# Summing attention weights over edges: VectorE adds half of every group's slots before TensorE's identity matmuls

## What is computed

```python
w_m = (efeat @ W_msg + b_msg).reshape(E, in_f, -1)     # [E, 16, 16]
w_a = (efeat @ W_attn + b_attn).reshape(E, in_f, -1)
h_src = feat[src][:, :, None]
e1, e2 = w_m * h_src, w_a * h_src
ex = jnp.exp(e2 - seg_max[dst])
denom = segment_sum(ex, dst)
ft = segment_sum(e1 * ex / denom[dst], dst)            # [N, 16, 16]
y = layernorm(x + ft.sum(axis=1))
out = layernorm(y + segment_mean(edge_attr, dst))
```

## Time and profile before

| what | us |
|---|---|
| median of 3 runs | 2243.48 (2243.09 to 2245.55) |
| span of the profiled execution | 2950.2 |
| busy in it: PE / PE weight loads / DVE | 2137.9 / 952.6 / 1862.0 |
| busy in it: ACT / POOL | 1256.9 / 1687.5 |
| mean granted TensorE clock in it | 0.861 |

### The profile page before, as it was taken

The page is one execution under the profiler, slowest core; times in us unless marked ns, Lnnn a source line. Parts: engine busy times, 40 slices in busy tenths (PEclk is TensorE's granted clock), DMA queues, the critical chain, the costliest instruction groups (busy, mean ns, idle before and its releaser), DMA issues. The chain is left out here.

```text
span 2950.2 us, 21765 instructions
## 1 busy us (share of the span) xinstructions
PE 2137.9 (72%) x6682; PEld 952.6 (32%) x6682; DVE 1862.0 (63%) x2907; ACT 1256.9 (43%) x1228; POOL 1687.5 (57%) x1845
## 2 busy tenths in 40 slices
PE   2347676676877777877787658877787767887777
PEld 1213233232333333333333223333333323333333
DVE  6246465566666666666676547766667656786776
ACT  3223443434444443454454325444444444554444
POOL 6556355665655565555565465655656565655633
PEclk8658888897988888989888889988989888988988
DMA  6000000000000000000000000000000001001000
GB/s 229 16 10 11 8 12 10 10 10 9 10 9 9 14 10 9 10 14 10 10 13 9 9 10 13 10 12 9 10 12 9 12 9 28 12 8 16 8 2 3
DMA packets 60073, 47.60 MB, mean 16 GB/s; under 512 B 28366, under 2 KB 55439, under 8 KB 59436
## 3 DMA queue, kind: packets, MB, share of 16 engines
q0 software_dynamic: 57632, 29.73, 8.0%
q1 hardware_dynamic: 2316, 16.38, 1.5%
HBM read 44.00 MB, written 1.90 MB: 16 GB/s over the span
## 5 line engine op out<-in xcount | busy, mean ns | idle before, releaser
L652 POOL DMA_INDIRECT AR<-in_xt,AR x1607 | 1538.8, 958 | 974.1 <-DVE AR L1472 491.3
L1128 PE MATMUL PX<-AR,CS 128*128 128x512 f32 x3246 | 1663.7, 642 | 37.8 <-issue 23.9
L1472 DVE CUSTOM_DVE_ANT_1 AR<-PW,AR 128x1024 f32<-128x1024 f32 x815 | 979.6, 1221 | 896.8 <-remote 651.2
L1108 PE MATMUL PW<-WS,LT 100*128 100x512 bf16 x1630 | 549.1, 423 | 683.9 <-DVE AR L1472 511.8
L1128 PEld LDWEIGHTS PX<-AR,CS 128*128 128x128 f32 x3246 | 664.9, 206 | 652.1 <-issue 532.4
L888 ACT ACTIVATE LT<-PTB 100x1024 bf16<-100x1024 bf16 (+1 forms) x221 | 211.2, 956 | 1005.7 <-remote 601.0
L1485 DVE TENSOR_TENSOR AR<-AR,PX 128x1024 f32<-128x1024 f32 (+1 forms) x442 | 501.0, 1134 | 121.3 <-ACT PX L944 76.0
L1108 PEld LDWEIGHTS PW<-WS,LT 100*128 100x128 bf16 x1630 | 141.5, 103 | 1113.7 <-DVE AR L1472 543.2
L946 ACT ACTIVATE AR<-AR 128x2048 f32<-128x2048 f32 (+1 forms) x221 | 412.9, 1869 | 7.2
L950 ACT ACTIVATE PX<-AR 128x1024 f32<-128x1024 f32 (+1 forms) x221 | 212.4, 961 | 412.3 <-DVE AR L1485 294.8
L944 ACT ACTIVATE PX<-AR 128x1024 f32<-128x1024 f32 (+1 forms) x221 | 231.0, 1045 | 39.4 <-DVE AR L1485 30.1
(11 more groups left out here) (192 smaller groups left out, 517.7 us busy)
## 6 DMA issues: line engine op xcount, KB each, us to landing
AR<-in_xt,AR POOLq DMA_INDIRECT x1607
AR<-in_eat SPq DMA_DIRECT2D x3, 3128.0 KB
AR<-in_eat SPq DMA_DIRECT2D x1, 3120.0 KB
y_d<-AR SPq DMA_DIRECT2D x1, 784.0 KB
AR<-y_d SPq DMA_DIRECT2D x1, 784.0 KB
AR<-in_es,E0I POOLq DMA_INDIRECT x48
y_d<-AR POOLq DMA_INDIRECT x36
CS<-in_cst SPq DMA_DIRECT2D x1, 442.0 KB, 5.3
```

The lines of the kernel that those rows point to most:

```text
L652: g.indirect_dma_start(feat(h, j - j0, j - j0 + 1), None, xt, bass.IndirectOffsetOnAxis(ap=node, axis=0)).then_inc(hg_sem(h), 16)
L1108: i = pe.matmul(PAIRS[s % 2][:, j, :], LT[:, g % 3, lo:lo + 128], WS[:, :], start=True, stop=True)
L1128: i = pe.matmul(PDR, IDN, x, start=(a == 0 and j == 0), stop=(g == LAST[k] and j == n - 1))
L1472: v.tensor_tensor_reduce(em(g, j, j + 2).rearrange("p (x c) -> p x c", c=32), w, hb, 1.0, LOW, ALU.mult, ALU.max, accum_out=MXC[:, k % 2, ...
```

## The change

`ADDS` goes: every group now has the `pairs` instruction. It also works on another set of slots. A group's slots are seen as two halves of 4 (or 3). In each half the first KEPT = 2 slots stay, and the rest (2 slots, or 1) is added to the first ones, in both halves by the same instruction, so 2 x 1024 elements for a group of eight and 2 x 512 for a group of six, in place in SBUF. TensorE then sums four slots for every group, one behind each of the four places of a step. It waits for `v_ad` of this group ahead of the first of them.

```diff
-ADDS = [c for p, c in STEPS[-8:] if p is None]
...
-                def gsum(g, lo, hi):
+                def gsum(g, x):
                     k, j0, n, a = GRP[g]
                     half = n // 2
...
+                    keep = KEPT(half)
+                    if x == 0:
+                        if a == 0 and k >= 1:
+                            pe.wait_ge(S["a_dn"], k)
+                        pe.wait_ge(S["a_exp"], g + 1)
+                        pe.wait_ge(S["v_ad"], g + 1)
+                    j = half * (x // keep) + x % keep
+                    y = em(g, j, j + 1).rearrange("p (i a o) -> p a i o", a=2, o=16)
+                    i = pe.matmul(PDR, IDN, y, start=(a == 0 and x == 0), stop=(g == LAST[k] and x == 2 * keep - 1))
+                    if x == 2 * keep - 1:
+                        i.then_inc(S["p_g"], 1)
...
-                            gsum(old, 2 * x, 2 * x + 2)
+                            gsum(old, x)
...
-                    sums = em(g, half, 2 * half - keep)
-                    v.tensor_tensor(sums, sums, em(g, half + keep, 2 * half), ALU.add).then_inc(S["v_ad"], 1)
+                    y = em(g).rearrange("p (h e) -> p h e", h=2)
+                    sums = y[:, :, 0:512 * (half - keep)]
+                    v.tensor_tensor(sums, sums, y[:, :, 512 * keep:512 * half], ALU.add).then_inc(S["v_ad"], 1)
...
                         gm(c, 1)
-                        if c in ADDS:
-                            pairs(c)
+                        pairs(c)
```

## The result

| | before | after |
|---|---|---|
| median, us | 2243.28 (2241.71 to 2245.55) | 2499.68 (2496.93 to 2501.39) |
| ratio | | **1.114**, 95% interval 1.1125 to 1.1156 |
| span of the profiled execution | 2950.2; a second profile, below: 2240.5 | 2499.6 |

The account below looks back on a forecast made before the run. GpSimd's gathers (2216 us) were taken to bound the kernel before, VectorE the changed one: 2314 busy plus 51 + 24 + 32 idle gives 2421, with 10 for TensorE's clock about 2430 us, range 2370 to 2510.

Parts of the forecast that it names:

- The "remote" waits: VectorE's mult in the first profile: 651.2 us of waits, taken to belong to the profiled execution, not the timed ones.
- GpSimd's floor of 2216 before: Kernel before: 1652 GpSimd issues at 1.25 us, last gather not before 2160, then about 6 and 50 us.
- 636 us less of TensorE: TensorE: 739 identity matmuls fewer at 0.86 us each; none of it comes off the time by itself.
- +452 us of VectorE: VectorE: 152 adds at 2.40 us and 69 at 1.34, less today's four adds.
- The sum 2421: VectorE in the changed kernel: 2314 us busy plus 51 + 24 + 32 idle that no overlap can fill.
- GpSimd's floor stays 2216, 205 below: GpSimd in the changed kernel: floor unchanged, its ring of 80 slots holds two batches, so nothing charged.
- The clock, +10: TensorE stands still over 3 us each step, so part of the steps run at half clock: +10 us.
- Half clock as the bound (2527): Rival: TensorE at half clock throughout becomes the changed kernel's bound, 2527 us; chance 0.08.
- Taking turns (2480): Rival: late gathers delay VectorE some 1 us in each of 49 batches, 2480 us; chance 0.07.
- No slower (2243): Rival: adds cheaper than priced fit in VectorE's idle time, so about 2243 us stays; chance 0.03.
- TensorE as the bound before (rival 4): TensorE at clock 0.86 set the time before, 2302 us; VectorE's 2421 still decides after; shares the forecast's 0.82.
- The signs that the prediction named: Profile after: adds' mean 1.96 us, VectorE busy near 2310, 1768 identity instructions, TensorE down over 600, GpSimd waiting longer.

Follow-up runs that it names:

- Relief alone: Kernel before, but TensorE sums only four slots of each group and no add runs; 2243.6 us, ratio 1.0005.
- the runs with fewer gathers: 1239 of 1607 gathers: kernel before 2153.14 us, changed kernel 2391.0, kernel before with four slots summed and no adds 1964.62.
- the PSUM input: Changed kernel with the add's second input read from PSUM instead of SBUF, same size, place and count; 2418.23 us, ratio 1.078.
- the adds alone: Changed kernel with its adds, but TensorE sums all 8 or 6 slots of a group again; 2512.44 us, ratio 1.1203.

## Why the prediction was right, and what it missed

The sign came for the reason given: VectorE has more to do and the relief of TensorE is worth nothing. The size is in the range in part by luck. The prediction had VectorE as the only bound of the changed kernel, and that path gives 2418 when nothing else disturbs it. The other 81 us come from gathers that are held up by the adds, which no term and no rival had; the room above 2430 that took them in was put there for other reasons (27 and 50 us). The low end has a slip of 10 us: 2430 - 42 - 8 is 2380, not 2370; nothing hangs on it.

**The "remote" waits.** Right: the second profile of the same kernel has a span of 2240.5 and none of them. Starting from each engine's own work instead of the span of 2950.2 was the step that made a forecast possible.

**GpSimd's floor of 2216 before.** Right. The last gather was forecast not before 2160 and starts at 2160.3. Relief alone and the runs with fewer gathers show that it is the bound. The 24 us by which the building ran short lie behind it: 80.2 us from the last gather to the end, where the prediction had 56.

**636 us less of TensorE are worth nothing.** Right in time (1.0005), though for this kernel alone: with room on GpSimd they are worth 186 us. As busy time they are less than thought, 1960.0 - 1617.0 = 343, since the instructions left run at a lower clock: identity instructions take 613 ns each instead of 478 (busy time over count, 1084.6 / 1768 and 1550.4 / 3246).

**+452 us of VectorE.** Nearly right. Busy 415 more, and 23.3 idle at the adds: 438. A large add took 2.29, the mean of all is 1961 ns where 1.96 was forecast. The 0.19 for waiting on gm is there too: 1504.46 - 1503.14 = 1.32. The Trainium skill's statement that this wait is free ("VectorE: DVE Perf Modes", The DRAIN you can't avoid) disagrees here as well, with 1.32 against the 1.13 of a free pair.

**The sum 2421.** As a sum of VectorE's own path it holds where nothing disturbs it: 2418.23 with the PSUM input. Part of that closeness is luck: VectorE's base was 10 us and the adds 14 us smaller than forecast, and its idle time larger.

**"GpSimd's floor stays 2216, 205 below ... I charge nothing for it."** This is the step that failed. The floor was built from a gather's pitch of 1.25 in a kernel that has no large add with two SBUF inputs, and was carried over as a constant. It rises by 241 us: 210 gathers that start inside an add take 2.16 instead of 0.944. The mirror of the failed step stands in the costing of the add: "L1383 reads PSUM, the new add does not ... no difference". That is right for the add's own duration and wrong for its neighbour: the PSUM input makes no difference to VectorE (1955 and 1961 ns) and 81 us to the kernel. With the 241 us up to the last gather GpSimd's sum is 2216 + 241 = 2457, above VectorE's 2421; the 24 us by which the tail was too short before and the 18 by which it grew make it 2499.

**The clock, +10.** The mechanism is there, its size is small. The step at 1514 of the changed kernel, on TensorE:

```profile
1513.79 1.02 PE L1121 MATMUL PX<-AR,CS 128*128 128x512 f32 x2
...
1518.72 1.04 PE L1107 MATMUL PW<-WS,LT 100*128 100x512 bf16 x2 [3.91 <-DVE AR L1464]
...
1519.55 1.91 PE L1121 MATMUL PX<-AR,CS 128*128 128x512 f32 x2
```

Behind the standstill of 3.91 us the W pair takes 1.04 and the two instructions of the identity matmul 1.91 instead of 1.02: half clock as in the earlier trace rows, and the granted clock from 1518.7 to 1521.5 is 0.50. Yet all mults together waited only 30.1 us for W pairs, since TensorE has so much room.

**The rivals.** Half clock as the bound (2527) is refuted by those 30.1 us and by the adds alone (mean clock 0.925, and no faster). Taking turns (2480) came nearest in time and had the right sign, "a batch whose gathers come late delays VectorE": `floors` waited 107.0 us for gathers, in 27 waits of up to 23.7. But it was held to be improbable because of 205 us of slack, and the held issues had eaten that. No slower (2243) is out. TensorE as the bound before (rival 4) is out by the relief alone, 1.0005.

**The signs that the prediction named.** The adds' mean, the 1768 identity instructions and the small waits for W came as written. VectorE busy was 2267.4 for 2310. TensorE's busy time was to fall by over 600 and fell by 343 (521 against the first profile). Two more signs failed together: VectorE was idle for 232 us outside of any "remote" wait, above the 200 that was set, and GpSimd did not wait longer for mult. Read together they say that VectorE hangs behind GpSimd, and not the reverse.

## What to carry to other kernels

Work that is moved to VectorE has a second price, on GpSimd: where indirect DMAs set the pace, count how many of them will start inside VectorE instructions that read both inputs from SBUF, and add for each what is left of that instruction. Here an input in PSUM took that price off (81 us), and instructions cut in two brought it down (62 us). And before an engine is relieved, find which engine sets the pace with one run that takes work from the suspect: 636 us of relief were worth 0 or 186 us, depending on it.

## What the runs showed of the hardware

- An indirect DMA issue of GpSimd that starts while VectorE runs an add with both inputs in SBUF lasts until about 0.82 us behind that add's end: 2.99 us instead of 0.94 for an add of 2.29. One that is under way when the add starts is not disturbed (180 of them, mean 0.945). With one input in PSUM it doesn't happen (321, mean 0.95), nor beside a reciprocal of 1.75 us with one SBUF input and an SBUF output (74, mean 0.944).
- A gap between instructions is not needed: two adds back to back let the held issue through at their boundary; the longest was 1.99 us, the mean of the 206 that started inside one (with some 0.12 us or more of it left) 1.45.
- A profiled execution can hold waits that the timed ones don't have: 651.2 us in one profile of a kernel, none in the next (2950.2 and 2240.5).
